# Sums of squares of two units in one VectorE reduction, and a hand-written order of the first layer with its projection one slot later

## The reference, cut to what matters

```
x = x + first_attention(layernorm(x))            # 16 heads of 8, window 32 with 16 on both sides
y = layernorm(x)
for i in range(6):                               # deep layers
    q, k, v = split(shift_tokens(y) @ Wqkv[i])   # 16 heads of 64
    q = l2norm(q) * qs ; k = l2norm(k) * ks      # needs the sum of squares of each head
    q, k = rotary(q), rotary(k)
    y = local_attention(q, k, v) @ Wo[i] + y
    y = (a * gelu(gate)) @ W2[i] + b2[i] + y     # a, gate from layernorm(shift_tokens(y)) @ W1[i]
x = x + y
```

## Time and profile before

| what | value |
|---|---|
| median of 3 runs | 3489.16 us (3488.1 to 3490.7) |
| profiled execution, its own time | 3491.41 us |
| span of its trace | 3489.3 us |
| PE, DVE, ACT, POOL busy | 97%, 92%, 89%, 78% |
| chain that ended last | PE 64%, POOL 14%, issue 11%, DVE 5%, ACT 5% |

### The profile page before, as it was taken

How to read it: one execution, slowest core, us unless ns; L and a number is a source line. 1 busy time by engine, 2 the same in 40 slices (tenths; PEclk the granted TensorE clock), 3 DMA queues, 4 the chain that set the end, 5 groups by cost and what they waited for, 6 DMA issues and landing times.

```text
span 3489.3 us, 109451 instructions
## 1 busy us (share of the span) xinstructions
PE 3392.9 (97%) x43104; PEld 2529.8 (73%) x43104; DVE 3225.9 (92%) x5281; ACT 3110.0 (89%) x5393; POOL 2727.2 (78%) x2652
## 2 busy tenths in 40 slices
PE   8998799999999999999999999999999999999997
PEld 6775577777777777777777777777777777777776
DVE  6886799999999999999999999999999999999994
ACT  5664699999999999999999999999999999999996
POOL 3333888888888888888888888888888888888782
PEclk9999899999999999999999999999999999999999
DMA  1000221221222122112212212221221222122121
GB/s 44 27 3 26 59 55 38 58 64 43 51 54 58 38 64 56 45 48 58 57 45 56 55 44 52 67 51 40 55 58 43 62 52 51 35 76 51 35 51 42
DMA packets 61707, 171.35 MB, mean 49 GB/s; under 512 B 9488, under 2 KB 21392, under 8 KB 60816
## 3 DMA queue, kind: packets, MB, share of 16 engines
q1 hardware_dynamic: 61200, 164.36, 18.5%
HBM read 21.72 MB, written 4.19 MB: 7 GB/s over the span
## 4 chain that ended last, share of the span: by engine, by line
PE 64%; POOL 14%; issue 11%; DVE 5%; ACT 5%; POOLq 0%; ACTq 0%; DVEq 0%
PE bank L1037 9%; PE bank L1361 7%; PE bank L1021 7%; PE bank L1002 6%; PE bank L969 6%; POOL rotbuf L1300 5%; PE bank L986 5%; PE bank L920 5%; PE bank L922 4%; PE bank L921 4%; POOL probs L1310 3%; POOL rotbuf L1286 3%; PE bank L360 2%; PE bank L380 2%; PE bank L345 2%
## 5 line engine op out<-in xcount | busy, mean ns | idle before, releaser
L1286 POOL TENSOR_TENSOR rotbuf<-mbuf 128x512 f32<-128x512 f32 x768 | 981.1, 1291 | 169.3 <-PE bank L969 151.0
L1300 POOL TENSOR_TENSOR rotbuf<-rotbuf,rs 128x512 f32<-128x512 f32 x768 | 788.1, 1046 | 14.9
L1310 POOL TENSOR_TENSOR probs<-probs,rden 128x768 f32<-128x768 f32 x384 | 563.5, 1468 | 91.0 <-DVE rden L1252 91.0
L1154 DVE TENSOR_REDUCE ss<-sq 128x8 f32<-128x512 f32 x768 | 522.1, 680 | 55.1 <-ACT sq L1063 46.2
L1173 DVE TENSOR_TENSOR mbuf<-bank,table 128x512 f32<-128x512 f32 x768 | 529.6, 690 | 23.5 <-DVE ss L1154 0.2
L1063 ACT ACTIVATE sq<-bank 128x512 f32<-128x512 f32 x768 | 456.1, 594 | 87.7 <-PE bank L922 77.6
L1174 DVE TENSOR_TENSOR mbuf<-bank,table 128x512 f32<-128x512 f32 x768 | 522.5, 680 | 0.0
L969 PE MATMUL bank<-ident,rotbuf 128*128 128x128 f32 x3072 | 478.7, 279 | 21.3 <-POOL rotbuf L1300 9.7
L1021 PEld LDWEIGHTS bank<-probs_t,vbuf 96*64 96x64 f32 x12288 | 390.1, 138 | 123.8 <-issue 75.0
L920 PE MATMUL bank<-weights,inputs 128*128 128x512 bf16 x1152 | 443.5, 385 | 22.8 <-DVE mbuf L1174 19.3
L1021 PE MATMUL bank<-probs_t,vbuf 96*64 96x64 f32 x12288 | 443.2, 225 | 1.4 <-ACT probs_t L1128 1.3
(11 more groups left out here) (115 smaller groups left out, 6232.2 us busy)
## 6 DMA issues: line engine op xcount, KB each, us to landing
vbuf<-v_stage SPq DMA_DIRECT2D x192, 384.0 KB, 4.5
vbuf<-v_stage SPq DMA_DIRECT2D x192, 256.0 KB, 3.7
vbuf<-v_stage SPq DMA_DIRECT2D x96, 128.0 KB, 4.5
stage<-in_wqkv SPq DMA_DIRECT2D x36, 256.0 KB, 5.2
weights<-in_wo SPq DMA_DIRECT2D x6, 512.0 KB, 6.7
out_t<-weights SPq DMA_DIRECT2D x1, 2048.0 KB, 6.3
weights<-out_t SPq DMA_DIRECT2D x1, 2048.0 KB, 9.4
out_t<-weights SPq DMA_DIRECT2D x16, 128.0 KB, 2.2
```

The costliest lines, as they stand in the source:

```text
L1286: e.tensor_tensor(b.rot[:, u, :], b.m1[:, u % 2, :], b.m2[:, u % 2, :], ALU.add).then_inc(s.rotated, 1)
L1300: e.tensor_tensor(v, v, r, ALU.mult).then_inc(s.scaled, 1)
L1310: e.tensor_tensor(probs, probs, b.rden[:, p % 2, :].unsqueeze(2).broadcast_to([P, 8, BLOCK_K]), ALU.mult).then_inc(s.probs, 1)
```

## The change

Two edits that do not touch each other.

**Deep layers.** One reduction now sums the squares of two units (1024 elements per partition into 16 columns) instead of one (512 into 8), so there are four per instance instead of eight. `sq` has four buffers instead of two, and a square waits for the pair two back. The rope of a unit no longer waits for its sum, but for its square. On DVE, the pair stands where the sum of its second unit stood; the sum of the first unit is taken out. The order is otherwise as it was.

**First layer.** New lists for all four engines and a new `FIRST_RING`. PE, for one, projects a sequence at the head of the next slot instead of right behind its last values.

```diff
 FIRST_RING = (
-    ("v", 1, -3), ("mean", 1, -4), ("mean", 0, 0), ("rstd", 0, -1), ("v", 0, -2),
-    ("q", 0, -1), ("out", 0, -3), ("k", 0, -1), ("rstd", 1, -4),
+    ("rstd", 1, -5), ("out", 0, -4), ("v", 1, -3), ("v", 0, -2), ("mean", 1, -4),
+    ("rstd", 0, -1), ("mean", 0, 0), ("k", 0, -1), ("q", 0, -1),
 )
...
 def pe_first_slot(e, s, b, at):
 
     pe_first_transpose(e, s, b, at, -3, 1)
+    pe_first_rstd(e, s, b, at, -5, 1)
+    pe_first_project(e, s, b, at, -4)
+    pe_first_v(e, s, b, at, -3, 1)
     pe_first_values(e, s, b, at, -3, 0)
-    pe_first_v(e, s, b, at, -3, 1)
-    pe_first_mean(e, s, b, at, -4, 1)
     pe_first_scores(e, s, b, at, -2, 0)
     pe_first_transpose(e, s, b, at, -3, 2)
+    pe_first_v(e, s, b, at, -2, 0)
+    pe_first_mean(e, s, b, at, -4, 1)
     pe_first_values(e, s, b, at, -3, 1)
+    pe_first_scores(e, s, b, at, -2, 1)
+    pe_first_variance(e, s, b, at, -4, 1)
+    pe_first_transpose(e, s, b, at, -3, 3)
+    pe_first_rstd(e, s, b, at, -1, 0)
     pe_first_mean(e, s, b, at, 0, 0)
-    pe_first_rstd(e, s, b, at, -1, 0)
-    pe_first_variance(e, s, b, at, -4, 1)
-    pe_first_scores(e, s, b, at, -2, 1)
-    pe_first_transpose(e, s, b, at, -3, 3)
+    pe_first_values(e, s, b, at, -3, 2)
+    pe_first_scores(e, s, b, at, -2, 2)
+    pe_first_k(e, s, b, at, -1)
+    pe_first_transpose(e, s, b, at, -2, 0)
+    pe_first_q(e, s, b, at, -1)
     pe_first_variance(e, s, b, at, 0, 0)
-    pe_first_v(e, s, b, at, -2, 0)
-    pe_first_values(e, s, b, at, -3, 2)
-    pe_first_q(e, s, b, at, -1)
-    pe_first_scores(e, s, b, at, -2, 2)
-    pe_first_transpose(e, s, b, at, -2, 0)
     pe_first_values(e, s, b, at, -3, 3)
-    pe_first_project(e, s, b, at, -3)
-    pe_first_k(e, s, b, at, -1)
     pe_first_scores(e, s, b, at, -2, 3)
-    pe_first_rstd(e, s, b, at, -4, 1)
...
 def act_square(e, s, b, at, ahead, u):
...
-    e.wait_ge(s.sq_summed, k.c[8] + (u - 1))
-    e.activation(b.sq[:, u % 2, :], work_bank(b, k, "pj", u)[:, :], ACT.Square).then_inc(s.pj_squared, 1)
+    e.wait_ge(s.sq_summed, k.c[4] + (u // 2 - 1))
+    e.activation(b.sq[:, u % 4, :], work_bank(b, k, "pj", u)[:, :], ACT.Square).then_inc(s.pj_squared, 1)
...
+def dve_sum_squares(e, s, b, at, ahead, pair):
...
+    col = 16 * pair
+    e.wait_ge(s.pj_squared, k.c[8] + (2 * pair + 2))
+    if pair == 0:
         e.wait_ge(s.clamped, k.c[1])
+    sq = b.sq[:, 2 * (pair % 2):2 * (pair % 2) + 2, :].rearrange("p u (h d) -> p (u h) d", h=8)
+    e.tensor_reduce(b.ss[:, col:col + 16], sq, AX_X, ALU.add).then_inc(s.sq_summed, 1)
...
 def dve_rope(e, s, b, at, ahead, u):
...
-    e.wait_ge(s.sq_summed, k.c[8] + (u + 1))
+    e.wait_ge(s.pj_squared, k.c[8] + (u + 1))
...
 def dve_deep_slot(e, s, b, at):
 
     dve_ff_refine(e, s, b, at, -2)
-    dve_sum_squares(e, s, b, at, 2, 0)
     dve_rope(e, s, b, at, 2, 0)
...
-    dve_sum_squares(e, s, b, at, 2, 1)
+    dve_sum_squares(e, s, b, at, 2, 0)
     dve_rope(e, s, b, at, 2, 1)
-    dve_sum_squares(e, s, b, at, 2, 2)
     dve_rope(e, s, b, at, 2, 2)
...
-    dve_sum_squares(e, s, b, at, 2, 7)
+    dve_sum_squares(e, s, b, at, 2, 3)
     dve_clamp(e, s, b, at, 2)
     dve_shift(e, s, b, at, 1, 0)
     dve_rope(e, s, b, at, 2, 7)
...
-        b.sq = sb("sq", [P, 2, 512])
+        b.sq = sb("sq", [P, 4, 512])
```

More of the change, by code:

```diff
@@ L81 @@
 FIRST_RING = (
[L82 to L83 removed]
+    ("rstd", 1, -5), ("out", 0, -4), ("v", 1, -3), ("v", 0, -2), ("mean", 1, -4),
+    ("rstd", 0, -1), ("mean", 0, 0), ("k", 0, -1), ("q", 0, -1),
 )
[L85 removed]
+FIRST_PE_REACH = (-5, 0)
 FIRST_ACT_REACH = (-4, 0)
[L87 to L88 removed]
+FIRST_DVE_REACH = (-5, 0)
+FIRST_POOL_REACH = (0, 0)
 LEAD = WINDOW // 2
@@ L652, in act_first_slot @@
+    act_first_copy_pt(e, s, b, at, -3, 2)
+    act_first_exp(e, s, b, at, -2, 0)
+    act_first_square(e, s, b, at, -4, 1)
+    act_first_copy_out(e, s, b, at, -3, 0)
+    act_first_v(e, s, b, at, -3, 1)
+    act_first_v(e, s, b, at, -2, 0)
+    act_first_copy_pt(e, s, b, at, -3, 3)
+    act_first_exp(e, s, b, at, -2, 1)
+    act_first_seed(e, s, b, at, -4, 1)
+    act_first_k(e, s, b, at, -1)
     act_first_square(e, s, b, at, 0, 0)
-    act_first_seed(e, s, b, at, -4, 1)
-    act_first_copy_pt(e, s, b, at, -3, 3)
@@ L655, in act_first_slot @@
-    act_first_seed(e, s, b, at, 0, 0)
-    act_first_exp(e, s, b, at, -2, 1)
+    act_first_copy_pt(e, s, b, at, -2, 0)
+    act_first_exp(e, s, b, at, -2, 2)
 def dve_first_slot(e, s, b, at):
+    dve_first_sum(e, s, b, at, -3, 1)
+    dve_first_max(e, s, b, at, -3, 2)
+    dve_first_shift(e, s, b, at, -3, 2)
+    dve_first_variance(e, s, b, at, -1, 0)
+    dve_first_refine(e, s, b, at, -5, 1)
+    dve_first_sum(e, s, b, at, -3, 2)
+    dve_first_max(e, s, b, at, -3, 3)
+    dve_first_shift(e, s, b, at, -3, 3)
@@ L661, in dve_first_slot @@
+    dve_first_norm(e, s, b, at, -5, 1)
+    dve_first_residual(e, s, b, at, -4)
+    dve_first_sum(e, s, b, at, -3, 3)
     dve_first_max(e, s, b, at, -2, 0)
     dve_first_shift(e, s, b, at, -2, 0)
-    dve_first_centre(e, s, b, at, 0, 0)
+    dve_first_centre(e, s, b, at, -4, 1)
+    dve_first_refine(e, s, b, at, -1, 0)
+    dve_first_sum(e, s, b, at, -2, 0)
+    dve_first_max(e, s, b, at, -2, 1)
+    dve_first_shift(e, s, b, at, -2, 1)
     dve_first_variance(e, s, b, at, -4, 1)
     dve_first_norm(e, s, b, at, -1, 0)
-    dve_first_sum(e, s, b, at, -2, 0)
@@ L680, in dve_first_slot @@
-    dve_first_centre(e, s, b, at, -3, 1)
-    dve_first_sum(e, s, b, at, -2, 3)
+    dve_first_centre(e, s, b, at, 0, 0)
 def pool_first_slot(e, s, b, at):
     pool_first_weights(e, b, at(0))
-    pool_first_normalise(e, s, b, at, -1, 2)
-    pool_first_normalise(e, s, b, at, -1, 3)
     pool_first_normalise(e, s, b, at, 0, 0)
     pool_first_normalise(e, s, b, at, 0, 1)
+    pool_first_normalise(e, s, b, at, 0, 2)
+    pool_first_normalise(e, s, b, at, 0, 3)
 def pe_first_layer(e, s, b):
@@ L1148, in dve_sum_squares @@
         return
-    t, isq, half = u // 4, (u // 2) % 2, u % 2
-    col = 2 * HEADS * t + HEADS * isq + 8 * half
-    e.wait_ge(s.pj_squared, k.c[8] + (u + 1))
-    if u == 0:
+    col = 16 * pair
+    e.wait_ge(s.pj_squared, k.c[8] + (2 * pair + 2))
+    if pair == 0:
         e.wait_ge(s.clamped, k.c[1])
-    e.tensor_reduce(b.ss[:, col:col + 8], b.sq[:, u % 2, :].rearrange("p (h d) -> p h d", h=8), AX_X,
-                    ALU.add).then_inc(s.sq_summed, 1)
+    sq = b.sq[:, 2 * (pair % 2):2 * (pair % 2) + 2, :].rearrange("p u (h d) -> p (u h) d", h=8)
+    e.tensor_reduce(b.ss[:, col:col + 16], sq, AX_X, ALU.add).then_inc(s.sq_summed, 1)
 def dve_rope(e, s, b, at, ahead, u):
@@ L1183, in dve_clamp @@
         return
-    e.wait_ge(s.sq_summed, k.c[8] + 8)
+    e.wait_ge(s.sq_summed, k.c[4] + 4)
     e.wait_ge(s.newton, k.c[REFINE_OPS])
@@ L1708, in dve_deep_slot @@
     dve_ff_gate(e, s, b, at, -2, 1)
-    dve_sum_squares(e, s, b, at, 2, 6)
     dve_rope(e, s, b, at, 2, 6)
```

32 lines of the change are left out of this document (5 added, 27 removed).

## The result

The changed kernel takes **3482.98 us** in the median of 13 runs (3479.52 to 3486.84), the kernel before 3489.22 (13 runs, 3486.26 to 3492.84): a ratio of 0.998, 95% interval 0.9972 to 0.9989. That is 6.2 us or 0.18% less, where 10 less were forecast. The sign is right and the size is near, but the forecast's terms are not what happened: the first layer gave 12.5 us by itself where 9.3 stood, and one deep slot in four became 0.79 us longer, which no step of the prediction had. The profiled execution took 3483.84 us with a span of 3482.0, so it stands 0.9 above its median, as the one of before stands 2.2 above its own.

What follows compares the result with a forecast made beforehand. It took PE, with a hole at the projection, to bound the first layer and a loop through POOL's chain the deep layers. Terms -9.3 + 0 + 0 - 1.5 = -10.8, rounded to -10, gave 3479 us, range 3465 to 3502.

Steps and rivals of the forecast that it cites:

- the prediction's own sign of being wrong: A deep slot off by over 0.05 us from 32.12, or another regular hole in the first layer, would show it wrong.
- where the clamp takes 0.35 instead of 0.50 us: Deep layers, every second slot or so: unit 7's rope ends 0.15 earlier; down projection starts 0.1 to 0.25 us late.
- a bound of +5: Deep layers: the pairs change nothing, 0, with ends of -10 to +5 us over 96 slots.
- 0.62 a slot: First layer: moving the projection one slot later removes PE's 0.62 us hole for sequences 0 to 14, 9.3 us.
- It adds to 18.1 to 18.2 us: First layer: the new PE list, with the old step lengths, gives a slot of 18.1 to 18.2 us.
- the fill and the end together within 1.5 either way: First layer: fill and end bounded by one hole or two either way, +-1.5 us, taken as 0.
- POOL's chain grows: Deep slots, rival: a moved DVE operation holds POOL once more, 0.2 us a slot, +19, 3498 us; chance 0.06.
- the faster rival: Deep slots: earlier ropes let POOL's chain start or run earlier, 0.15 us a slot, -14, 3465 us; chance 0.13.
- The rope of unit 1: Deep slots: transpose of unit 2 0.36 us late, within 0.46 slack; rival: does not fit, 3502 to 3503, chance 0.13.
- Last layer: Nine slots with the outer operation: rope 0.2 us later, about as much given back; 0, ends -4 and +2.
- Between the parts: From 330 to 440 us, while the deep pipeline fills: -1.5 us, ends -6 and +2.
- The rule weighed: Optimise the engine with highest occupancy first: DVE edit worth nothing in deep layers, no harm; sum -9.3, 3480 us.

Runs made afterwards that it cites:

- The ninth experiment: Changed kernel without clamp, feed-forward root's operation moved to PSUM, rotation of unit 1 ahead of the sum of squares of units 0 and 1: 3458.57 us, ratio 0.9911.

## Why the prediction was right, and where it was wrong

The sum, -10 against a measured -6.2, came out by errors that cancelled: the first layer and the last one gave more than was put down, the slots with a weight piece lost what nothing was put down for. That the number came out near is luck: by the prediction's own sign of being wrong, a deep slot off by over 0.05 us, every kind of deep slot was.

**The clamp is where it failed.** The step reads "where the clamp takes 0.35 instead of 0.50 us, as it does in every second slot or so, the rope ends 0.15 earlier". I took the clamp's duration as a property of the slot (it is 0.35 us in the 29 slots with a piece of the table above, and 0.50 in the others). It is the time until a POOL operation lets go, and the edit moved the clamp by 0.53 us. In plain slots that took it out of the normalisation (0.50 to 0.20 us), so that the down projection, forecast 0.1 to 0.25 late, began as before (4.67 us into the slot for 4.68, its second matmul 0.05 late). In slots with a piece it moved the clamp over the start of the normalisation. The rows of before held it: 1533.46 - 1533.21 = 0.25 us was all that parted the clamp from being second. A quarter of the slots went up by 0.79 us, +19.0 in all, against a bound of +5 for everything in the loop. The Trainium skill (SBUF — State Buffer, section Who interferes with whom) states it outright: a `tensor_scalar` in its two-port mode and GpSimd take a shared pair of ports in turn, "the other fully blocks", and a `tensor_reduce` on this chip never does. The traces agree on both, 1.24 and 0.22 us in the same place. I had cited that section, but only for the feed-forward operations, where a hold had looked partial.

**First layer: the mechanism right, the size too small.** 0.62 a slot was the term; the move alone gives 0.55, the whole edit 0.92. "It adds to 18.1 to 18.2 us" used the old steps for the new neighbours, and the transposes' step depends on them. From projection 0 to 15 the gain is 15.9 us, where -9.3 stood; 3.6 of it come in the last interval, and the prediction had the fill and the end together within 1.5 either way. The runs keep 12.5 of it. Why the last interval fell by so much no run here takes apart.

**The plain slot: the named risk, with the other sign.** "POOL's chain grows" said that the moved root could lie over two short POOL operations instead of one. It left the first (0.49 to 0.29) and touched the second for only 0.07 (0.32 to 0.39): -0.15 a slot and -7.9 us, inside the ends of -10 to +5 but not the 0 I took. It moved by 0.22 us and not by 0.4 (from 4.72 to 4.94 us into the slot), because the clamp in front of it gave back 0.30. The place given to the faster rival (ropes letting POOL begin earlier) was wrong; POOL begins at the same 4.8 us behind the mean.

**The rope of unit 1: right in plain slots.** Forecast 0.36 us late with 0.46 of slack; measured 0.26, and nothing behind it moved. In the once-a-layer slots it does cost: +0.22 us in five slots, given back when the rotation went first. The ninth experiment shows no slack there at all, and I never looked at those slots by themselves.

**Last layer: under-sized.** The term was 0 with ends of -4 and +2, and it gave -4.3. Before, PE waited 0.82 us for the rotation behind the outer operation; the prediction had that rotation 0.2 us later in the change, and the transpose stands 0.57 us earlier in the slot (13.07 for 13.64). One sum less in front of it starts the outer operation 0.62 us earlier (6.87 for 7.49), and being held for less it takes 0.47 less; the longer pair takes 0.53 of the 1.09 back. So relieving DVE did pay here, but nearly half of it came by the port, and the outer operation, whose cost the prediction read as 0.57 us a slot, spent 0.85 of its 1.27 us held by POOL.

**Between the parts** -1.5 was forecast. The profile pair gives -0.7, but the runs with pairs have 110.1 to 113.9 us there and those without 114.6 to 115.5, so about -3 is nearer.

**The rule weighed.** The prediction read PE, at 99%, as the engine with the highest occupancy. The Trainium skill (Perfetto Trace Analysis, section Identifying the Most-Contended Engine) does not take matmul busy time as the measure for TensorE, but the arithmetic done against the peak, and the busy time of its weight loads. The weight loads are 2136 of 2900 us, 74%, so by them DVE, at 96%, comes first and the rule speaks for the pairs. The deep half of the change followed it, and cost 6.75 us.

## What to carry to other kernels

An operation's duration in a profile may be a wait for a port. Before an edit moves a short SBUF-to-SBUF operation, look at what the neighbouring engine runs at its old and at its new time, and ask by how little it was first: losing 0.25 us of lead cost 0.8 us in each such slot. Where DVE and GpSimd both work all the time, put such an operation into a form that leaves the shared port alone (a reduction, another engine, one operand in PSUM), and judge an edit by the kinds of slot apart, since a mean over them hid +19 and -8.

## What the runs showed of the hardware that I had not expected

The holds can be read to a few hundredths of a microsecond. A `tensor_scalar` on 64 columns was held until 0.15 us before the recorded end of the POOL operation (normalisation, piece or cast: three cases). The same 0.15 fits the plain slots of before (held from 1501.09 to 1501.39, the normalisation's end at 1501.53) and the outer operation, held behind POOL's scaling: its 1.27 and 0.80 us follow from its own 0.42 to 0.01 us. The other way round, a DVE operation on 256 columns with two SBUF inputs, 0.42 us long, held a POOL operation until 0.28 us after its own start: before, 1504.02 + 0.28 = 1504.30, and POOL's 0.50 less its own 0.29 from 1504.09 is 1504.30; in the change, 1495.45 + 0.28 = 1495.73, and the second refinement (0.39 instead of 0.32, from 1495.66) gives 1495.73; without the clamp, 1484.79 both ways. So this hold was not partial, as I had thought: it is whole for the first 0.28 us, and the rest of the recorded 0.42 holds nobody. Whether 0.28 us is the time in which the operation reads, no run shows.

The step from a group of transposes to the next group on PE is 0.97 to 1.01 us when values follow and 0.87 to 0.92 when others do, with no wait shown by the profile; what makes the difference stays open.
